# First 432 tiles of relation edges gathered as plain rows beside the making of the relation table

## The reference

```python
hx = jnp.einsum('ni,rio->rno', x, weight)          # x is layernorm(x) here
msg = hx[edge_type, src]                            # 200000 edges
agg = jax.ops.segment_sum(msg, dst, num_segments=num_nodes)
node_repr = agg * 0.5 ** 0.5 + h_bias + (x @ loop_weight) * 0.5 ** 0.5
```

## Time and profile before

| what | us |
|---|---|
| median of 3 runs (5589.6 to 5602.57) | 5592.78 |
| the profiled execution, its own time | 5587.87 |
| its span in the trace | 5586.1 |
| PE busy, share of the span | 82% |
| POOL busy | 59% |
| DVE busy | 46% |
| ACT busy | 27% |

### The profile page before, as it was taken

The page is one execution under the profiler, slowest core; times in us unless marked ns, Lnnn a source line. Parts: engine busy times, 40 slices in busy tenths (PEclk is TensorE's granted clock), DMA queues, the critical chain, the costliest instruction groups (busy, mean ns, idle before and its releaser), DMA issues. The chain is left out here.

```text
span 5586.1 us, 72963 instructions
## 1 busy us (share of the span) xinstructions
PE 4589.4 (82%) x18025; PEld 2918.7 (52%) x18026; DVE 2560.5 (46%) x8476; ACT 1535.1 (27%) x3400; POOL 3321.6 (59%) x3405
## 2 busy tenths in 40 slices
PE   3998888887888788963588888876769999997698
PEld 1554333333333333323477777765347777775466
DVE  6562333333333222233355555544875544444682
ACT  1332000000000000001244444434467644442132
POOL 1113777777777777750477777770357777776121
PEclk9998555566656655555699999987889999998798
DMA  3323333333333433320333323225155544443001
GB/s 138 128 122 132 105 105 105 105 105 106 105 105 109 108 105 105 105 76 11 69 61 61 61 60 60 60 54 186 63 153 174 162 136 137 134 136 101 13 1 46
DMA packets 312438, 545.32 MB, mean 98 GB/s; under 512 B 74735, under 2 KB 212734, under 8 KB 305810
## 3 DMA queue, kind: packets, MB, share of 16 engines
q0 software_dynamic: 141088, 319.86, 22.1%
q1 hardware_dynamic: 171092, 222.51, 12.3%
HBM read 449.02 MB, written 93.08 MB: 97 GB/s over the span
## 5 line engine op out<-in xcount | busy, mean ns | idle before, releaser
L959 PE MATMUL e_sums<-e_ring,e_onehot 128*128 128x257 f32 x3136 | 1660.2, 638 | 307.8 <-DMA e_ring<-table,erow 225.1
L713 POOL DMA_INDIRECT e_ring<-table,erow x1568 | 1490.8, 951 | 477.9 <-issue 381.3
L959 PEld LDWEIGHTS e_sums<-e_ring,e_onehot 128*128 128x128 f32 x3136 | 734.3, 287 | 1228.9 <-issue 907.1
L1901 POOL DMA_INDIRECT t_source<-source_rows,t_index x848 | 808.5, 953 | 271.0 <-issue 232.2
L1070 POOL DMA_INDIRECT e_ring<-table,esrc x800 | 802.9, 1004 | 243.6 <-issue 156.1
L914 DVE SCALAR_TENSOR_TENSOR big<-e_sums,within,big 128x257 f32 x196 | 95.1, 485 | 1289.9 <-PE e_sums L959 1289.9
L1146 PE MATMUL e_total<-e_loads,e_times 128*128 128x256 f32 x2176 | 536.2, 381 | 0.0
L1157 PE MATMUL e_sums<-e_ring,e_onehot 128*128 128x256 f32 x1600 | 449.5, 391 | 81.1 <-DMA e_ring<-table,esrc 76.0
L2050 PE MATMUL t_raw<-big,t_w 128*128 (+1 forms) x1600 | 428.1, 428 | 8.6 <-issue 8.6
L1146 PEld LDWEIGHTS e_total<-e_loads,e_times 128*128 128x128 f32 x2176 | 399.0, 190 | 65.7
L920 DVE TENSOR_SCALAR e_onehot<-ramp,edst 128x128 f32<-128x128 f32 x1568 | 344.4, 294 | 95.3 <-PEq L106 67.3
(11 more groups left out here) (382 smaller groups left out, 5365.4 us busy)
## 6 DMA issues: line engine op xcount, KB each, us to landing
table<-r_stage SPq DMA_DIRECT2D x49, 1024.0 KB
e_loads<-table SPq DMA_DIRECT2D x384, 128.0 KB
t_near<-near_rows SPq DMA_DIRECT2D x106, 256.0 KB
e_ring<-table,erow POOLq DMA_INDIRECT x1568
m_outputs<-first_outputs SPq DMA_DIRECT2D x49, 512.0 KB, 4.8
first_outputs<-t_stage SPq DMA_DIRECT2D x96, 256.0 KB
t_source<-source_rows,t_index POOLq DMA_INDIRECT x848, 2.4
e_ring<-table,esrc POOLq DMA_INDIRECT x800
```

What stands on the lines that cost most here:

```text
L713: eng.indirect_dma_start(ring[:, t % BODY, 0:D], None, table, bass.IndirectOffsetOnAxis(ap=b.erow[:, t:t + 1], axis=0)).then_inc(gathered[ ...
L959: eng.matmul(sums[g % SUMS][:, 0:ACCW], onehot[t % ONEHOTS][:, :], ring[:, t % BODY, :], start=(t % GROUP == 0), stop=(t % GROUP == GROUP ...
L1901: eng.indirect_dma_start(source[s][:, q, :], None, a.source_rows, bass.IndirectOffsetOnAxis(ap=index[s][:, q:q + 1], axis=0)).then_inc(gat ...
```

## The change

The first 432 tiles (`EARLY`, 55296 edges) leave `relation_sums` and are done inside `relation_table`, by another way. The normalised rows are written over x in SBUF and stored as plain rows `rows1` (6272 by 256). POOL no longer normalises; it gathers 432 tiles out of `rows1` into a ring of 8. The place of an edge is now its target within a window of 16 nodes, times 8, plus its relation, so that a sum row stands for one target and one relation; 4 tiles make a group. PE takes two such tiles behind each product, from window 5 on; the matrices of zeros and ones are made by DVE for even tiles and by ACT for odd ones; DVE adds each group to two windows of `b.x`, cleared for it, and to `b.counted`, and does one step of the sort at each odd tile.

In `relation_sums` 1136 tiles are left. Between its tiles 8 to 102, in 48 parts (`put`), the 48 windows of sums are transposed, multiplied by the eight weights and added to the accumulator, after which x is loaded again. `attention_inputs` is written out without loops, four buffers deep, with one copy instead of two on ACT and all 16-column products of a half in one bank. Weights are loaded in `constants`, which also has the windows of the early groups to work out.

```diff
-FILLED = 6
+FILLED = 9
-RANGED = 6
+RANGED = 15
-EDGED = 10
+EDGED = 20
+EARLY = 432
+EGROUP = 4
+EGROUPS = EARLY // EGROUP
+ENODES = P // RELS
+EWINDOWS = 48
 def constants(nc, b, m):
...
+            for k in range(KH):
+                eng.dma_start(b.weights[:, k, :, :], m["weight"][:, k * P:(k + 1) * P, :].rearrange("r p o -> p r o")).then_inc(b.weighted, 16)
...
 def relation_table(nc, b, m):
...
+    BANKS = 3
+    RUN = 7
+    MINE = 4
+    DIRECT = 6
+    HELD = 3
+    RING = 8
+    STARTS = 5
+    PERBODY = 10
+    early_at = lambda w, c: [t for t in range(PERBODY * (w - STARTS) + 2 * c, PERBODY * (w - STARTS) + 2 * c + 2) if 0 <= t < EARLY]
...
+            for j in range(NW // RUN):
+                eng.wait_ge(normed[0], MINE * (j + 1))
+                eng.wait_ge(normed[1], (RUN - MINE) * (j + 1))
+                eng.dma_start(runs[j], b.x[:, RUN * j:RUN * (j + 1), :]).then_inc(written, 16)
+            eng.wait_ge(written, 16 * (NW // RUN))
...
-            for w in range(NW):
-                wait_if(eng, transposed, w - 1)
-                eng.tensor_scalar(xn[w % 2][:, :], b.x[:, w, :], b.mean[:, w:w + 1], b.rstd[:, w:w + 1],
-                                  ALU.subtract, ALU.mult).then_inc(normed, 1)
+            eng.wait_ge(written, 16 * (NW // RUN))
+            eng.sem_inc(cleared, 1)
+            for t in range(EARLY):
+                if t >= RING:
+                    eng.wait_ge(summed, t - RING + 1)
+                    eng.sem_inc(cleared, 1)
+                eng.indirect_dma_start(ring[:, t % RING, 0:D], None, m["rows1"], bass.IndirectOffsetOnAxis(
+                    ap=b.esrc[:, t:t + 1], axis=0)).then_inc(gathered[t % RING], 16)
...
+            for _ in range(TABLE_FIRST):
+                next(sort_steps)
+            eng.wait_ge(written, 16 * (NW // RUN))
+            eng.wait_ge(transposed, DIRECT)
+            eng.memset(b.x[:, :, :], 0.0).then_inc(zeroed, 1)
...
+            for t in range(EARLY):
+                if t % 2 == 0:
+                    wait_if(eng, summed, t - RING + 1)
+                    eng.tensor_scalar(onehot[t % RING][:, :], b.ramp[:, 0:P], b.edst[:, t:t + 1], None,
+                                      ALU.is_equal).then_inc(matched[0], 1)
+                else:
+                    next(sort_steps, None)
+                if t % EGROUP == EGROUP - 1 and t // EGROUP >= 1:
+                    add(t // EGROUP - 1)
...
+            for w in range(NW):
+                eng.wait_ge(copied, w + 1)
+                if w + 1 < NW:
+                    turn(w + 1)
+                for c in range(OUTS):
+                    multiply(w, c)
+                    for t in early_at(w, c):
+                        gather_sum(t)
+                        if t in FLIPPED:
+                            flip(FLIPPED.index(t))
...
 def relation_sums(nc, b, m, table):
...
-    SUMS = 4
+    SUMS = 2
+    TILES = NT - EARLY
+    CHUNKS = EWINDOWS * ENODES // P
+    FILLS = RELS // 2
+    PUTS = 2 * FILLS
+    PUT = lambda n: BODY // 2 + 2 * n
+    put_at = {PUT(n): divmod(n, PUTS) for n in range(CHUNKS * PUTS)}
...
+            def put(c, f):
+                if f < FILLS:
+                    wait_if(eng, laid, c * FILLS + f)
...
+                            mm = eng.transpose(turning[:, (2 * k + two) * P:(2 * k + two + 1) * P],
+                                               b.x[:, c * RELS + 2 * f + two, k * P:(k + 1) * P], b.ident[:, :])
...
-            for t in range(NT):
+            for t in range(TILES):
...
+                if t in put_at:
+                    put(*put_at[t])
...
 def attention_inputs(nc, b, m, a):
+    WAYS = 4
+    AHEAD = 2
...
+            for w in range(AHEAD):
+                turn(w)
+            for w in range(NW):
+                if w + AHEAD < NW:
+                    turn(w + AHEAD)
```

More of the change, by code:

```diff
@@ L375, in relation_table @@
         kept = sem("r_kept")
+        cleared = sem("r_cleared")
+        gathered = [sem(f"r_gathered{s}") for s in range(RING)]
+        parted = sem("r_parted")
+        matched = [sem(f"r_matched{s}") for s in range(2)]
+        summed = sem("r_summed")
+        added = sem("r_added")
         block = ctx.enter_context(nc.Block())
@@ L506, in flip, with gather_sum @@
+            def gather_sum(t):
+                g = t // EGROUP
+                if t % EGROUP == 0:
+                    wait_if(eng, added, 4 * (g - 1))
+                eng.wait_ge(matched[t % 2], t // 2 + 1)
+                eng.wait_ge(gathered[t % RING], 16 * (t // RING + 1))
+                eng.matmul(sums[g % 2][:, 0:ACCW], onehot[t % RING][:, :], ring[:, t % RING, :],
+                           start=(t % EGROUP == 0), stop=(t % EGROUP == EGROUP - 1)).then_inc(summed, 1)
             def flip(n):
@@ L548, in both, with evacuate @@
-            def both(w, s):
-                if not (isinstance(w, int) and w == NW - 1):
-                    body(w + 1, 1 - s)
-                evacuate(w, s)
-            body(0, 0)
-            each_window(eng, both)
+            def evacuate(w, c):
+                n = OUTS * w + c
+                eng.wait_ge(multiplied, n + 1)
+                if c == 0:
+                    wait_if(eng, stored[w % 2], 16 * (w // 2))
+                if c < OUTS - 1:
+                    eng.activation(stage[w % 2][:, c * BANK:(c + 1) * BANK], product[n % BANKS][:, :],
+                                   ACT.Copy).then_inc(evacuated, 1)
+                else:
+                    eng.activation(b.acc[:, w, 0:D], product[n % BANKS][:, 0:D], ACT.Copy).then_inc(evacuated, 1)
@@ new lines, in match @@
+            def match(t):
+                n = t // 2
+                wait_if(eng, matched[1], n - 1)
+                eng.activation(away[n % 2][:, :], b.ramp[:, 0:P], ACT.Abs, bias=b.edst[:, t:t + 1], scale=-1.0).then_inc(parted, 1)
+                wait_if(eng, summed, t - RING + 1)
+                eng.wait_ge(parted, n + 1)
+                eng.activation(onehot[t % RING][:, :], away[n % 2][:, :], ACT.Relu, bias=b.ones[:, 0:1],
+                               scale=-1.0).then_inc(matched[1], 1)
@@ new lines, in _ @@
+            for w in range(NW):
+                if w % RUN >= MINE:
+                    eng.activation(b.x[:, w, :], b.x[:, w, :], ACT.Identity, bias=b.shift[:, w:w + 1],
+                                   scale=b.rstd[:, w:w + 1]).then_inc(normed[1], 1)
+            copy(0)
+            for w in range(NW):
+                if w + 1 < NW:
+                    copy(w + 1)
+                for c in range(OUTS):
+                    evacuate(w, c)
+                    t = PERBODY * (w - STARTS) + 2 * c + RING - 1
+                    if 0 <= t < EARLY:
+                        match(t)
@@ L1165, in _, with far_edges @@
                         inner(g)
-def far_edges(nc, b, table, rows, use, reach):
+def far_edges(nc, b, table, rows, use, reach, targets):
     with Phase(nc) as ctx:
@@ L2320, in _ @@
             eng.wait_ge(loaded, 32)
[L2321 removed]
+            eng.wait_ge(brought, 112)
         @block.gpsimd
```

608 lines of the change are left out of this document (392 added, 216 removed).

## The result

| kernel | us, median (lowest to highest) | runs | against before |
|---|---|---|---|
| before | 5591.19 (5588.86 to 5602.57) | 4 | 1 |
| changed | 5259.94 (5255.98 to 5262.44) | 4 | 0.9403, 95% interval 0.9387 to 0.9419 |

The change takes 331 us off, where 368 were forecast; 5225 us was predicted, and the range of 5160 to 5310 holds the time. The profiled execution of the changed kernel took 5259.42 us, its span 5257.3.

A forecast was written before the change was run, and what follows sets the result against it. The prediction took POOL's gather issue rate to bound the sums and PE the table's stage; -542 + 219 + 10 - 55 = -368 us from 5587.9 gave 5220, as a median 5225 us, range 5160 to 5310.

The forecast's parts named there:

- What bounds the sums, and that 432 tiles of them are gone: Edge sums: POOL's gather issue rate, 1.255 us a tile, is the limit; 432 fewer tiles take off 542 us.
- POOL sets the pace of the early tiles: Table's stage: gathers at 1.32 us a tile, bounds 1.255 to 1.64; 424 of them take 560 us.
- the two cases in the earlier trace: Gathers beside DVE instructions: 1.17 us at L752 (two SBUF inputs), 1.33 at L742 and L743 (one each), against 0.946.
- The sign I gave for the second rival: Early tiles in the table's stage: a median gather over 1.1 us would speak for POOL held up by wide DVE instructions.
- second rival: Early tiles: POOL held up by each wide DVE instruction, 1.60 us a tile, +119 us, 5344 us; chance 0.08.
- The first rival: Early tiles: the chain of four engines loses time, 1.45 us a tile, +55 us, 5280 us; chance 0.15.
- PE at full clock beside POOL: Table's stage: PE about 93% loaded at a clock near 1.00, one window with ten early tiles taking 12.25 us.
- the fifth rival: Table's stage: PE falls to 1.2 GHz waiting for tiles, +486 us, 5711 us; chance 0.03 together with the far path.
- The start: Start of the table's stage: `constants` takes 6 us more for loads and DVE instructions, so 84 instead of 78.2 us.
- The way to tile 0: Table's stage, from its start at 84 us to the first early tile on PE at 150 us: 66 us.
- The parts: The 48 parts in the sums: 10 us, bounds 0 and 86, with PE's clock expected to rise under load.
- The attention's inputs: Attention's inputs: unchained windows at half clock and fewer copies, -55 us, the stretch 65 us long.

The follow-up runs named there:

- the experiment with two SBUF inputs: Changed kernel plus two unused 512-column DVE instructions, both inputs in SBUF, at each odd early tile from 353 on: 5267.4 us in one execution.
- the ring of 14: Changed kernel with a ring of 14 gathered tiles instead of 8 in the table's stage: 5249.3 us in one execution.
- the sort through PSUM: Changed kernel with the sort's second input copied by ACT to PSUM beside early tiles, two product banks instead of three: 5209.32 us, 0.9313 of before.
- The two extra-instruction kernels: Changed kernel plus two unused DVE instructions per odd tile from 353, with two SBUF inputs or one SBUF and one PSUM: 5267.4 and 5247.5 us.

## Why the prediction was right, and where it was off

- **What bounds the sums, and that 432 tiles of them are gone**: right. 1.255 us a gather before and 1.262 after, -534.5 us for -532. The 0.007 us more on each of 1136 gathers are 8 us; the forecast had 10, all of them for the parts.
- **POOL sets the pace of the early tiles**: right, as the waits and the experiment with two SBUF inputs show. The term was mis-sized: 1.32 us a tile, 1.365 measured. I put an excess of 0.14 us on half of the gathers from the two cases in the earlier trace rows. The share was about right, 184 of 432 overlap such an instruction, but their excess is 0.27 us; the mean over all is 0.115 to 0.118, by the base taken. The sign I gave for the second rival, a median over 1.1 us, would have missed this: the median is 0.949. The earlier trace rows had shown one instruction of 1.23 us, and the trace has only short ones of 128 columns behind it. The sort has unbroken runs of instructions, and by the timeline above a gather that finds no gap waits through several; the longest took 2.25 us. A tile costs 0.11 us more than the unhindered 1.255; the forecast had 0.065 and the second rival, whose mechanism it is, 0.345. The first rival, 1.45 us by the chain of engines, is refuted by the ring of 14 and by the sort through PSUM, which has a further hand-over and is faster. I read both cases of the earlier trace rows as one thing, though the greater excess stood beside instructions with a single SBUF input.
- The Trainium skill, SBUF — State Buffer, section Who interferes with whom, says which pairs block each other, and two SBUF inputs against a read of GpSimd is one of them; an instruction with at most one SBUF input is free of it as long as it runs in none of DVE's two-port performance modes. The two extra-instruction kernels (1.046 and 0.947 us) agree on both halves; which mode the instructions of the neighbour layer ran in, no trace here says. Its rule that the loser blocks to the end of the instruction explains the 2.05 us only if POOL also loses the gaps between DVE's instructions; no run here looked inside a gather.
- **PE at full clock beside POOL, the fifth rival's subject**: right, 0.99 in [160, 745], 95% busy.
- **The start**: the step that failed is "+6 us, so this stage starts at 84". It started at 92.5, 14.3 us later than before; 6.45 of these are the small stores that are read back by way of DRAM, for which the prediction had nothing. They were in the code of the change and I counted only loads and DVE instructions.
- **The way to tile 0**: 66.6 us for 66 is luck, two errors of opposite sign.
- **The parts**: the forecast's 10 us were 4.7, and the clock was high there as assumed (0.94).
- **The attention's inputs**: right, 56.9 us in the trace and 52.5 by themselves for 55. The clock stayed at 0.50 with PE busy 58 of 62 us.
- **The 6 us behind** lie outside the sums and the attention's inputs. The neighbours' gathers take 4 us of them (1049.1 against 1045.4), in an unchanged stage, and these are held-up gathers again: adding up what each takes over 0.946 us gives 49.7 us against 46.1. In all ten profiles here the stage is 999.3 to 999.5 us and this sum, which goes from 43.0 (the attention's part alone, 1042.3 us) to 53.0. How the gathers fall on DVE's instructions differs from one execution to the next. The other 2 us stay open.

## What to carry to other kernels

Before moving gathers beside other work, list the DVE instructions that will run beside them and count those with two SBUF operands, and with them the wide and fast ones with a single one: their share of the time, and whether they come in unbroken runs, sets what a gather costs, while as many two-input instructions with one operand in PSUM cost nothing. Judge it by the mean gather, not by the median. If an engine is idle anyway, a copy of one operand to PSUM buys the gathers' time back. And a small table that goes out to DRAM and comes back puts microseconds on the path of whoever reads it (7.2 us for three stores here, 13.65 for six), however few bytes it has.

## What the runs showed of the hardware

- A gather of 128 rows holds POOL for 0.946 us and follows the one before at 1.255; beside DVE instructions with two SBUF inputs it took up to 2.25 us, and the DVE instructions were not longer for it (0.683 us with 512 columns at L389 beside gathers, 0.685 at L321 with none).
- Beside one-input DVE instructions of 512 columns, 0.88 us for two, gathers of the neighbour layer took 1.187 us on the average and up to 2.53.
- The same DVE instruction with its second input in PSUM takes as long (0.683 against 0.688 us) and doesn't touch the gather (0.947 us, where 0.946 is the median of the earlier trace rows).
- PE's clock was 0.63 at 94.9 us busy of 117, where it waited for gathers, and 0.94 at 103.6 busy in the same stretch with the parts between; the parts cost some 5 us. In the attention's inputs it was 0.50 (1.2 GHz) at 57.9 busy of 62 us.
- A DVE clearing of 128x12544 fp32 took 10.5 us, where a sum of that size took 13.2.
